# A fused macaron block on one Trainium2 core: second norm of the first feed-forward phase on ScalarE, transposes in halves, k weight split first

## The chip, the cores and the metric

The kernel runs on one core of a Trainium2 chip. The metric is the device time of one execution in microseconds (us). Three runs of the kernel before took 5574.15, 5580.31 and 5580.04 us; their median is 5580.04.

## The reference, cut to what matters

The input x is (4, 2048, 512) in float32. Three blocks follow one another, each on a layer norm of its input:

```python
x = x + 0.5 * ffn(layernorm(x))      # first feed-forward phase
x = x + mixer(layernorm(x))          # state-space block with its own residual
x = x + 0.5 * ffn(layernorm(x))      # second feed-forward phase, same weights
...
def ffn(x):                          # x_prev is x one token earlier, zero at a sequence's start
    xr = mu_r * x + (1 - mu_r) * x_prev
    xk = mu_k * x + (1 - mu_k) * x_prev
    r = sigmoid(xr @ W_r.T)
    k = square(relu(xk @ W_k.T))
    return r * (k @ W_v.T)
```

The mixer returns its output plus its own (normalised) input. So its residual is x1 + h2, where x1 is what the first feed-forward block gives and h2 is the layer norm of x1. The mixer centres its input and multiplies by W_in; then come a short convolution, a selective scan over 16 states and an output product.

## The kernel before

The program has three parts, one after the other: `ffn_phase` named "f1", `mixer_phase`, and `ffn_phase` named "f2". All engines meet at the end of each part. Inside a part each engine runs its own instruction list, written out by hand, and waits on semaphores; an engine executes its list strictly in order. So the order of calls in each engine's function is the schedule.

**A feed-forward phase** handles 16 chunks of 512 tokens (FT; four a sequence). A chunk lies as four tiles of 128 tokens by 512 channels. Its steps, with the engine and the line:

- SP (SyncE) loads x (line 171) and stores the result (197); it also stores h2T, the transposed second norm, for the mixer (204).
- VectorE does `norm1` (343 to 357): statistics, then rstd from POOL (`power`, 223), then the normalised hx. TensorE turns hx (`turn1`, 476) into two PSUM banks `ps_t`, four blocks one after the other, and ScalarE copies each block to xhT (271). POOL takes the difference to the token before (`shift`, 231, one instruction over the whole chunk). VectorE mixes (375), ScalarE makes the rounded high part (278 for xk, 285 for xr), and VectorE the low part (378).
- TensorE makes the products k, r and v, each as three matmuls on high and low parts (509 to 511), 48 for each of k, r and v in a chunk. ScalarE takes relu, square and the high part of k (291 to 295) and the tanh of r (303); VectorE makes k's low part (390), multiplies r by v (422) and adds into x (427). That sum is x1.
- Only in f1: a second norm of x1 on VectorE (343 to 357 again, output h2), the sum x1 + h2 on POOL (247), TensorE's transposes of h2 (`turn2`, 476, all four blocks, through the same two banks) and ScalarE's copies to h2T (333).

The work is software-pipelined. In the body of chunk i TensorE runs v of chunk i, the transposes of hx of chunk i+2, k and r of chunk i+1, and the transposes of h2 of chunk i. VectorE runs x1 and the second norm of chunk i, k's low part of chunk i+1, the xk mix of i+2, norm1 of i+3 and the xr mix of i+2. ScalarE runs the xhT copies (i+2), the k tiles and two r tiles (i+1), xk's high part (i+2), two r tiles (i+1), the four h2T copies (i) and xr's high part (i+2). The last three bodies leave out the chunks that don't exist. In the last body of f1 TensorE and VectorE also centre W_in for the mixer (399, 560); a tile named mx_w_in in the trace can be one that f1 uses as scratch for x, hx, the difference or the mix.

**The prologue** of each phase loads chunk 0 of x, then W_r, W_k and W_v and the two mu vectors (164 to 169). TensorE transposes the three weights block by block into the two `ps_t` banks (466, twelve groups), ScalarE copies out the high part (258) and VectorE subtracts for the low part (406). That happens after the transposes of chunk 0 and ahead of the first mix. The fourth chunk of x is loaded only once all weights are transposed, since W_v waits in its buffer (172).

Of the kernel before, what the change touches and what calls it, by code (L numbers as in the profile page):

```python
# [14 lines left out]
F32 = mybir.dt.float32  # L15
# [35 lines left out]
def ffn_phase(nc, name, x_in, w_r, w_k, w_v, mu_r, mu_k, out, hT_pad=None, ahead=None):  # L51
# [7 lines left out]
    with ExitStack() as ctx:  # L59
# [25 lines left out]
        rstd = sb("rstd", [P, 2, FJ])  # L85
        mark = sb("mark", [P, 1])
# [20 lines left out]
        s_w = sem("weights_loaded")  # L107
# [11 lines left out]
        s_dsh = sem("dsh_ready")  # L119
        s_mk = sem("xk_mixed")  # L120
# [13 lines left out]
        s_xs = sem("xs_ready")  # L134
        s_t2 = sem("h2_transposed")
# [8 lines left out]
        block = ctx.enter_context(nc.Block())  # L144

# [17 lines left out]
        def _(sp):  # L163
            sp.dma_start(x[0][:, :, :], x_v[0]).then_inc(s_x[0], 16)
            for n, w in enumerate((w_r, w_k, w_v)):
                sp.dma_start(w_nat[n], w.rearrange("(o p) c -> p o c", p=P)).then_inc(s_w, 16)
            for n, m in enumerate((mu_r, mu_k)):
                sp.dma_start(mu[:, n, :], m.rearrange("(o p) -> p o", p=P),
                             allow_slow_non_contiguous=True).then_inc(s_w, 16)
# [41 lines left out]
        def _(pool):  # L211
# [42 lines left out]
        def _(act):  # L254
            def copy_weights():
                for g in range(3 * NB):
                    act.wait_ge(s_wt, g + 1)
                    nc.scalar.activation(w_hi[:, g // NB, g % NB, :], ps_t[g % 2][:, :], ACT.Copy).then_inc(s_wh, 1)  # L258
# [28 lines left out]
            def copy_k(i):  # L287

                for d in range(NB):
# [1042 lines left out]
```

## Time and profile before

| what | value |
|---|---|
| runs, us | 5574.15, 5580.31, 5580.04; median 5580.04 |
| the profiled execution's own time | 5575.4 us |
| its span, first to last instruction | 5573.6 us |
| mean granted TensorE clock | 0.990 of full |
| TensorE busy (matmul) | 5397.0 us, 97% |
| VectorE busy | 4949.2 us, 89% |
| POOL busy | 4269.2 us, 77% |
| ScalarE busy | 3482.6 us, 62% |
| first feed-forward phase | 0 to about 706 us |
| mixer | about 706 to 4943 us |
| second feed-forward phase | from about 4943 us |

All times in the rows are microseconds from the start of the span, unless marked ns. A busy engine isn't always at its peak: an instruction that waits for a port or for another engine's hold on it counts as busy too. PE is TensorE, DVE VectorE, ACT ScalarE, POOL GpSimd, SP SyncE; L427 is line 427 of the kernel before.

### The profile page before, as it was taken

The page shows a single profiled execution, that of the slowest core. Times are in us where ns is not written, and L with a number is a line of the kernel's source. Part 1 is how long each engine was busy: PE and PEld are TensorE (multiplying, and loading weights), DVE is VectorE, ACT ScalarE, POOL GpSimd, SP SyncE. Part 2 cuts the span into 40 slices and gives each one's busy share as a digit, 9 for nine tenths or more (in the row PEclk, how much of TensorE's full clock was granted, in tenths as well). Part 3 has the DMA queues.
Part 4 walks back from the last instruction along what each step waited for, and adds up shares of the span by engine and source line. Part 5 has one row for each costly group of instructions (what it writes and reads, how often), then busy time and mean ns, then how long its engine had stood idle before and what let it go on. Part 6 is the DMA issues. An engine that isn't in the chain of part 4 may idle for free. (4 is left out here: it accounts for less than half of the span.)

```text
span 5573.6 us, 82586 instructions
## 1 busy us (share of the span) xinstructions
PE 5397.0 (97%) x23584; PEld 4365.6 (78%) x23584; DVE 4949.2 (89%) x8180; ACT 3482.6 (62%) x8814; POOL 4269.2 (77%) x2671
## 2 busy tenths in 40 slices
PE   7999989999999999999999999999999999979999
PEld 6777768888777788878878888777788888857777
DVE  6888779999999999999999999999999999966775
ACT  4444357677666766766766677666766766744443
POOL 2233269999999999999999999999999999931110
PEclk8999999999999999999999999999999999989999
DMA  2212221111111111111111111111111111121111
GB/s 85 91 68 89 81 103 35 43 50 58 56 44 43 43 43 43 43 43 46 43 43 43 43 51 57 57 43 43 43 43 43 43 43 46 43 95 61 53 53 46
DMA packets 140105, 298.00 MB, mean 53 GB/s; under 512 B 23424, under 2 KB 41888, under 8 KB 139680
## 3 DMA queue, kind: packets, MB, share of 16 engines
q1 hardware_dynamic: 139680, 293.09, 15.4%
q8 instruction: 174, 2.85, 0.2%
q14 instruction: 251, 2.06, 0.1%
HBM read 223.79 MB, written 69.27 MB: 53 GB/s over the span
## 5 line engine op out<-in xcount | busy, mean ns | idle before, releaser
L845 POOL TENSOR_TENSOR mx_dbu<-mx_bs,mx_du 128x1024 f32<-128x1024 f32 x1024 | 2414.8, 2358 | 39.2 <-POOL mx_du L838 28.9
L973 ACT ACTIVATE mx_ps_da<-mx_dl,mx_a 128x256 f32<-128x256 f32 x4096 | 1775.5, 464 | 82.7 <-DVE mx_hp L1052 48.2
L1052 DVE TENSOR_TENSOR_SCAN mx_hp<-mx_ps_da,mx_hst,mx_dbu 128x256 f32<-128x256 f32 x2048 | 1500.8, 733 | 0.3 <-ACT mx_ps_da L973 0.3
L1052 DVE TENSOR_TENSOR_SCAN mx_ps_da<-mx_ps_da,mx_hst,mx_dbu 128x256 f32<-128x256 f32 x2048 | 1416.9, 737 | 11.1 <-ACT mx_ps_da L973 6.1
L826 POOL TENSOR_TENSOR mx_hp<-mx_hp,mx_cs 128x512 f32<-128x512 f32 x1024 | 1303.7, 1273 | 4.1 <-ACT mx_hst L907 4.1
L1207 PE MATMUL mx_ps_y<-mx_hp,mx_ident 128*128 128x256 f32 x4096 | 1054.3, 380 | 0.0
L1198 PE MATMUL mx_ps_y<-mx_hc,mx_ident 128*128 128x256 f32 x4096 | 1051.1, 379 | 0.0
L1174 PE MATMUL mx_ps_m<-mx_u,mx_w_dt 128*128 128x256 f32 x4128 | 936.6, 380 | 5.6 <-issue 5.6
L1207 PEld LDWEIGHTS mx_ps_y<-mx_hp,mx_ident 128*128 128x128 f32 x4096 | 774.0, 190 | 174.6 <-issue 60.4
L1174 PEld LDWEIGHTS mx_ps_m<-mx_u,mx_w_dt 128*128 128x128 f32 x4128 | 786.5, 191 | 113.9 <-issue 6.3
L925 ACT ACTIVATE mx_hst<-mx_ps_da 128x2 f32<-128x2 f32 x1022 | 173.6, 170 | 1103.8 <-DVE mx_hc L1064 1099.7
L1198 PEld LDWEIGHTS mx_ps_y<-mx_hc,mx_ident 128*128 128x128 f32 x4096 | 778.2, 190 | 105.8
L1064 DVE TENSOR_TENSOR mx_hc<-mx_ps_da,mx_cs 128x512 f32<-128x512 f32 x1024 | 688.7, 673 | 137.6 <-PE mx_ps_y L1198 132.2
L1155 PE MATMUL mx_ps_m<-mx_hT,mx_w_in 128*128 128x256 f32 x2072 | 501.6, 385 | 56.6 <-DVE mx_u L1024 56.6
L1147 PE MATMUL mx_ps_m<-mx_hT,mx_w_in 128*128 128x259 f32 x2136 | 514.1, 383 | 5.0 <-PEq L59 3.7
L223 POOL TENSOR_TENSOR f_rstd<-f_ve,f_half 128x4 f32<-128x4 f32 x48 | 48.5, 1011 | 606.5 <-DVE f_ve L352 606.2
L1147 PEld LDWEIGHTS mx_ps_m<-mx_hT,mx_w_in 128*128 128x128 f32 x2136 | 406.1, 190 | 122.6 <-issue 63.6
L1155 PEld LDWEIGHTS mx_ps_m<-mx_hT,mx_w_in 128*128 128x128 f32 x2072 | 390.0, 191 | 135.3 <-DVE mx_u L1024 82.5
L1186 PE MATMUL mx_ps_m<-mx_w_out,mx_gy 128*128 128x512 f32 x1024 | 480.6, 592 | 0.8 <-DVE mx_xo L1043 0.8
L1024 DVE SCALAR_TENSOR_TENSOR mx_u<-mx_ps_m,mx_cw,mx_u 128x256 f32<-128x256 f32 x798 | 379.5, 476 | 18.3
L817 POOL TENSOR_TENSOR mx_dl<-mx_dl,mx_en 128x256 f32<-128x256 f32 x257 | 186.8, 727 | 172.7 <-ACT mx_en L901 171.1
L1186 PEld LDWEIGHTS mx_ps_m<-mx_w_out,mx_gy 128*128 128x128 f32 x1024 | 194.5, 190 | 138.9 <-issue 124.1
(107 smaller groups left out, 6745.1 us busy)
## 6 DMA issues: line engine op xcount, KB each, us to landing
mx_bs<-bc_scratch SPq DMA_DIRECT2D x132, 512.0 KB, 3.7
mx_cs<-bc_scratch SPq DMA_DIRECT2D x132, 512.0 KB, 3.9
mx_hT<-hT_scratch SPq DMA_DIRECT2D x34, 518.0 KB, 3.9
hT_scratch<-f_h2T SPq DMA_DIRECT2D x16, 1024.0 KB, 5.1
mx_xo<-xs_scratch SPq DMA_DIRECT2D x32, 512.0 KB, 5.1
x_scratch<-mx_xo SPq DMA_DIRECT2D x32, 512.0 KB, 5.1
f_x<-x_scratch SPq DMA_DIRECT2D x16, 1024.0 KB, 5.7
out_dram<-f_x SPq DMA_DIRECT2D x16, 1024.0 KB, 4.2
```

Of the source, the lines that this page charges most:

```text
L826: G.tensor_tensor(h, h, cs[:, g, SD:SG, :], ALU.mult).then_inc(s_pr, 1)
L845: G.tensor_tensor(dbu[:, n % NM], bs[:, g], bcast(du[:, b % 2, :], SG), ALU.mult).then_inc(s_m1, 1)
L973: ins = A.activation(ps_da[DA_BANK[p]][:, k, :], dl[:, b % NL, :], ACT.Exp, scale=a_sb[:, b, s:s + 1])
L1024: V.scalar_tensor_tensor(out=q, in0=in_bank(b)[:, step:step + T], scalar=cw[:, step, b:b + 1], in1=q, op0=ALU.mult, op1=ALU.add).then_inc( ...
L1052: ins = V.tensor_tensor_scan(da if half == 0 else hp[:, n % NH, k, :], da, dbu[:, n % NM, s, :], hst[:, b, SG * g + s:SG * g + s + 1], ALU ...
L1064: V.tensor_tensor(hc[:, n % NC, :, :], ps_da[DA_BANK[2 * n]][:, :, :], cs[:, g, 0:SD, :], ALU.mult).then_inc(s_m2, 1)
L1147: ins = M.matmul(in_bank(b)[:, 0:TH], w_in_sb[:, f, b * P:(b + 1) * P], hT[cp][:, f, :], start=(f == 0), stop=(f == NB - 1))
L1155: ins = M.matmul(m_bank(b)[:, 0:T], w_in_sb[:, f, DI + b * P:DI + (b + 1) * P], hT[cp][:, f, PAD_L:PAD_L + T], start=(f == 0), stop=(f == ...
L1174: ins = M.matmul(m_bank(b)[:, 0:T], w_dt_sb[:, k, b * P:(b + 1) * P], u[:, cp, k, :], start=(k == 0), stop=(k == ND - 1))
L1186: ins = M.matmul(ps_c[:, :], gy[:, cp, b, j * P:(j + 1) * P], w_out_sb[:, b, :], start=(b == 0), stop=(b == ND - 1), skip_group_check=True)
L1198: ins = M.matmul(ps_y[b % 2][:, 0:T], ident[:, :], hc[:, n % NC, k, :], start=(g == 0 and k == 0), stop=False, skip_group_check=True)
L1207: ins = M.matmul(ps_y[b % 2][:, 0:T], ident[:, :], hp[:, n % NH, k, :], start=False, stop=(g == NG - 1 and k == SG - SD - 1), skip_group_c ...
```

## The change

In both phases the k weight is loaded and split first, ahead of the transposes of chunk 0. Two of the r weight's blocks are transposed before k's first two tiles and two after them; the v weight comes after k's last tile. The shift, the xk mix and its rounding are done block by block for chunk 0. The mu loads stand ahead of those of W_r and W_v on SP's queue. In the first phase VectorE computes only the statistics of the second norm and two small factors, shift2 = -mean x rstd and gain2 = rstd + 1. ScalarE computes h2 = rstd x x1 + shift2, and in place x = gain2 x x1 + shift2, which is x1 + h2. POOL's sum is gone. The transposes of h2 come in two halves, one between r's second and third tile, one after r's last. In the last body ScalarE makes the sum last.

```diff
+        shift2 = sb("shift2", [P, FJ])
+        gain2 = sb("gain2", [P, FJ])
...
+        W_ORDER = (1, 0, 2)
+        def groups(nth, of=range(NB)):
+            return [(NB * nth + o, W_ORDER[nth], o) for o in of]
...
-            for n, w in enumerate((w_r, w_k, w_v)):
-                sp.dma_start(w_nat[n], w.rearrange("(o p) c -> p o c", p=P)).then_inc(s_w, 16)
+            sp.dma_start(w_nat[1], w_k.rearrange("(o p) c -> p o c", p=P)).then_inc(s_w[1], 16)
             for n, m in enumerate((mu_r, mu_k)):
                 sp.dma_start(mu[:, n, :], m.rearrange("(o p) -> p o", p=P),
-                             allow_slow_non_contiguous=True).then_inc(s_w, 16)
+                             allow_slow_non_contiguous=True).then_inc(s_mu, 16)
+            sp.dma_start(w_nat[0], w_r.rearrange("(o p) c -> p o c", p=P)).then_inc(s_w[0], 16)
+            sp.dma_start(w_nat[2], w_v.rearrange("(o p) c -> p o c", p=P)).then_inc(s_w[2], 16)
...
                 pool.wait_ge(s_tc, NB * (i + 1))
                 pool.wait_ge(s_prev, i + 1)
-                if not (isinstance(i, int) and i == 0):
-                    pool.wait_ge(s_xr, i)
+                pool.wait_ge(s_xr, i)
                 nc.gpsimd.tensor_tensor(dsh[:, :, :], xhT[:, slot, :, 1:FT + 1], xhT[:, slot, :, 0:FT],
                                         ALU.subtract).then_inc(s_dsh, 1)
+            def first_shift():
+                pool.wait_ge(s_prev, 1)
+                for f in range(NB):
+                    pool.wait_ge(s_tc, f + 1)
+                    nc.gpsimd.tensor_tensor(dsh[:, f, :], xhT[:, 0, f, 1:FT + 1], xhT[:, 0, f, 0:FT],
+                                            ALU.subtract).then_inc(s_dsh0, 1)
             def prologue():
                 power(0, 0)
-                shift(0, 0)
+                first_shift()
...
-                    pool.wait_ge(s_h2, FJ * (i + 1))
-                    nc.gpsimd.tensor_tensor(x[c][:, :, :], x[c][:, :, :], h2[:, :, :], ALU.add).then_inc(s_xs, 1)
...
-            def copy_weights():
-                for g in range(3 * NB):
+            def copy_weights(nth, of=range(NB)):
+                for g, n, o in groups(nth, of):
                     act.wait_ge(s_wt, g + 1)
-                    nc.scalar.activation(w_hi[:, g // NB, g % NB, :], ps_t[g % 2][:, :], ACT.Copy).then_inc(s_wh, 1)
+                    nc.scalar.activation(w_hi[:, n, o, :], ps_t[o % 2][:, :], ACT.Copy).then_inc(s_wh, 1)
+            def first_high_xk():
+                for f in range(NB):
+                    act.wait_ge(s_mk, f + 1)
+                    nc.scalar.activation(xk_hi[:, f, :], mix[:, f, :], ACT.Copy).then_inc(s_hi0, 1)
...
+            def second_norm(i, c):
+                act.wait_ge(s_nb, i + 1)
+                for j in range(FJ):
+                    nc.scalar.activation(h2[:, j, :], x[c][:, j, :], ACT.Identity, bias=shift2[:, j:j + 1],
+                                         scale=rstd[:, 1, j:j + 1]).then_inc(s_h2, 1)
+            def add_second_norm(i, c):
+                for j in range(FJ):
+                    ins = nc.scalar.activation(x[c][:, j, :], x[c][:, j, :], ACT.Identity, bias=shift2[:, j:j + 1],
+                                               scale=gain2[:, j:j + 1])
+                ins.then_inc(s_xs, 1)
+            def copy_h2T(i, blocks):
+                for f in blocks:
+                    act.wait_ge(s_t2, NB * i + f + 1)
+                    nc.scalar.activation(h2T[:, f, 0:FT], ps_t[f % 2][:, :], ACT.Copy).then_inc(s_t2c, 1)
             def prologue():
                 act.wait_ge(s_id, 3)
+                copy_weights(0)
                 copy_xhT(0, 0, True)
-                copy_weights()
-                high_xk(0)
+                first_high_xk()
+                copy_weights(1, range(2))
                 high_xr(0)
-                copy_k(0)
+                copy_k(0, range(2))
+                copy_weights(1, range(2, NB))
+                copy_k(0, range(2, NB))
+                copy_weights(2)
                 copy_xhT(1, 1, False)
                 high_xk(1)
...
                     copy_k(i + 1)
+                if mixer:
+                    second_norm(i, c)
                 if left == 0 or left > 1:
                     copy_r(i + 1, range(2))
+                if mixer:
+                    if left != 1:
+                        add_second_norm(i, c)
+                    act.wait_ge(s_ht, (2 * BATCH + 1) * 16 + 16 * i)
+                    copy_h2T(i, range(2))
                 if left == 0 or left > 2:
                     high_xk(i + 2)
                 if left == 0 or left > 1:
                     copy_r(i + 1, range(2, FJ))
                 if mixer:
-                    act.wait_ge(s_ht, (2 * BATCH + 1) * 16 + 16 * i)
-                    for f in range(NB):
-                        act.wait_ge(s_t2, NB * i + f + 1)
-                        nc.scalar.activation(h2T[:, f, 0:FT], ps_t[f % 2][:, :], ACT.Copy).then_inc(s_t2c, 1)
+                    copy_h2T(i, range(2, NB))
+                    if left == 1:
+                        add_second_norm(i, c)
                 if left == 0 or left > 2:
                     high_xr(i + 2)
...
+            def split_weights(nth, of=range(NB)):
+                for g, n, o in groups(nth, of):
+                    dve.wait_ge(s_wh, g + 1)
+                    V.tensor_tensor(w_lo[:, n, o, :], ps_t[o % 2][:, :], w_hi[:, n, o, :].bitcast(F32),
+                                    ALU.subtract).then_inc(s_wc, 1)
+            def first_mixed_k():
+                dve.wait_ge(s_mu, 2 * 16)
+                for f in range(NB):
+                    dve.wait_ge(s_dsh0, f + 1)
+                    V.scalar_tensor_tensor(out=mix[:, f, :], in0=dsh[:, f, :], scalar=mu[:, 1, f:f + 1],
+                                           in1=xhT[:, 0, f, 0:FT], op0=ALU.mult, op1=ALU.add).then_inc(s_mk, 1)
+                for f in range(NB):
+                    dve.wait_ge(s_hi0, f + 1)
+                    ins = V.tensor_tensor(xk_lo[:, f, :], mix[:, f, :], xk_hi[:, f, :].bitcast(F32), ALU.subtract)
+                ins.then_inc(s_xk, 1)
             norm1(0, 0, 0, 1)
-            dve.wait_ge(s_w, 5 * 16)
-            for g in range(3 * NB):
-                dve.wait_ge(s_wh, g + 1)
-                V.tensor_tensor(w_lo[:, g // NB, g % NB, :], ps_t[g % 2][:, :],
-                                w_hi[:, g // NB, g % NB, :].bitcast(F32), ALU.subtract).then_inc(s_wc, 1)
-            mixed_k(0, 0)
+            split_weights(0)
+            first_mixed_k()
+            split_weights(1, range(2))
             mixed_r(0, 0)
+            split_weights(1, range(2, NB))
             norm1(1, 1, 1, 1)
+            split_weights(2)
             split_k(0)
             mixed_k(1, 1)
             norm1(2, 2, 2, 1)
...
-                    def free():
-                        if left in (1, 2):
-                            dve.wait_ge(s_t2, NB * i)
-                            dve.wait_ge(s_xs, i)
-                    norm(1, x[c], h2, norms_before_2(i, left), s_h2, free)
+                    statistics(1, x[c], norms_before_2(i, left))
+                    if not (isinstance(i, int) and i == 0):
+                        dve.wait_ge(s_xs, i)
+                    V.scalar_tensor_tensor(out=shift2[:, :], in0=mv[:, 1, :, 0], scalar=-1.0, in1=rstd[:, 1],
+                                           op0=ALU.mult, op1=ALU.mult)
+                    V.tensor_scalar(gain2[:, :], rstd[:, 1], 1.0, None, ALU.add).then_inc(s_nb, 1)
...
-            def turn_weights():
-                for g in range(3 * NB):
-                    if g >= 2:
+            def turn_weights(nth, of=range(NB)):
+                for g, n, c in groups(nth, of):
+                    if c == 0:
+                        pe.wait_ge(s_w[n], 16)
+                    if c >= 2 or nth == 2:
                         pe.wait_ge(s_wc, g - 1)
-                    else:
-                        pe.wait_ge(s_tc, NB)
+                    elif nth == 1:
+                        pe.wait_ge(s_tc, NB - 1 + c)
                     for o in range(NB):
-                        ins = M.transpose(ps_t[g % 2][:, o * P:(o + 1) * P],
-                                          w_nat[g // NB][:, o, (g % NB) * P:(g % NB + 1) * P], ident[:, :])
+                        ins = M.transpose(ps_t[c % 2][:, o * P:(o + 1) * P],
+                                          w_nat[n][:, o, c * P:(c + 1) * P], ident[:, :])
                     ins.then_inc(s_wt, 1)
...
+                    elif isinstance(i, int) and i < 2:
+                        pe.wait_ge(s_wc, (2 * i + 1) * NB - 1 + f)
...
+                turn_weights(0)
                 turn1(0)
-                pe.wait_ge(s_w, 5 * 16)
-                turn_weights()
-                k_products(0)
+                turn_weights(1, range(2))
+                k_products(0, range(2))
+                turn_weights(1, range(2, NB))
+                k_products(0, range(2, NB))
+                turn_weights(2)
...
-                    r_products(i + 1)
+                    r_products(i + 1, range(2))
                 if mixer:
-                    turn2(i)
+                    turn2(i, range(2))
+                if left == 0 or left > 1:
+                    r_products(i + 1, range(2, FJ))
+                if mixer:
+                    turn2(i, range(2, NB))
```

## Rows read from the trace of the kernel before

**Rows 1.** Busy time by stretch: start:end, length, then per engine busy and count, clock, DMA.

```profile
core 0: us, PE busy (x) PEld busy (x) DVE busy (x) ACT busy (x) POOL busy (x), PEclk, DMA share, GB/s
123.55:161.85 38.30, 37.73 (x177) 30.42 (x176) 30.40 (x51) 17.98 (x27) 11.73 (x4) 1.00 0.22 83
...
279.40:319.74 40.34, 37.71 (x177) 30.43 (x176) 33.75 (x51) 17.78 (x27) 12.41 (x4) 1.00 0.21 78
...
5100.46:5136.42 35.96, 35.71 (x163) 28.75 (x161) 25.29 (x37) 15.84 (x23) 4.61 (x2) 1.00 0.17 59
85.30:645.60 560.30, 532.95 (x2459) 429.85 (x2458) 461.81 (x686) 249.86 (x377) 170.36 (x55) 0.99 0.21 77
```

**Rows 2.** Timeline of TensorE: start, length, engine, line, operation, operands, count, idle before.

```profile
304.13 1.04 PE L476 MATMUL f_ps_t<-f_ident,f_h 128*128 128x128 f32 x8
307.54 1.15 PE L476 MATMUL f_ps_t<-f_ident,f_h 128*128 128x128 f32 x8 [2.37 <-ACT f_h2T L333]
308.44 0.47 PE L509 MATMUL f_ps_v<-f_w_lo,f_ka_hi 128*128 128x512 f32 x1
...
319.76 1.04 PE L476 MATMUL f_ps_t<-f_ident,mx_w_in 128*128 128x128 f32 x8
...
321.95 0.47 PE L509 MATMUL f_ps_kr<-f_xk_lo,f_w_hi 128*128 128x512 f32 x1
```

**Rows 3.** Timeline of VectorE over the same body.

```profile
288.54 2.47 DVE L346 BATCH_NORM_STATS2 f_stats<-f_x 128x6 f32<-128x512 f32 x4
...
291.46 0.17 DVE L352 TENSOR_SCALAR f_ve<-f_mv 128x4 f32<-128x4 f32 x1
292.75 1.92 DVE L356 TENSOR_SCALAR f_h<-f_x,f_mv,f_rstd 128x512 f32<-128x512 f32 x4 [1.12 <-POOL f_rstd L223]
...
297.00 7.08 DVE L375 SCALAR_TENSOR_TENSOR mx_w_in<-mx_w_in,f_mu,f_xhT 128x512 f32<-128x512 f32 x4
...
321.40 2.47 DVE L422 SCALAR_TENSOR_TENSOR f_rt<-f_rt,f_ps_v 128x512 f32<-128x512 f32 x4
323.91 4.95 DVE L427 SCALAR_TENSOR_TENSOR f_x<-f_rt,f_x 128x512 f32<-128x512 f32 x4
```

**Rows 4.** Timeline of POOL over the same body.

```profile
294.75 6.79 POOL L247 TENSOR_TENSOR f_x<-f_x,f_h 128x2048 f32<-128x2048 f32 x1 [2.03 <-DVE f_h L356]
...
322.90 3.60 POOL L231 TENSOR_TENSOR mx_w_in<-f_xhT 128x2048 f32<-128x2048 f32 x1 [10.46 <-ACT f_xhT L271]
```

**Rows 5.** Timeline of ScalarE over the same body.

```profile
294.36 0.64 ACT L295 ACTIVATE f_ka_hi<-f_ka 128x512 fp32r<-128x512 f32 x1
...
304.11 1.91 ACT L278 ACTIVATE f_xk_hi<-mx_w_in 128x2048 fp32r<-128x2048 f32 x1 [4.82 <-DVE mx_w_in L375]
```

**Rows 6.** Groups of ScalarE, whole run: shapes, count, busy, mean ns, idle before.

```profile
L973 ACT ACTIVATE mx_ps_da<-mx_dl,mx_a 128x256 f32<-128x256 f32 x4096 | 1775.5, 464 | 82.7 <-DVE mx_hp L1052 48.2
...
L901 ACT ACTIVATE mx_en<-mx_en 128x256 f32<-128x256 f32 x258 | 103.2, 400 | 0.1
...
L303 ACT ACT_TABLE_LOAD x1 | 1.3, 1283 | 0.0
```

**Rows 7.** Chain that ended last, prologue of the second phase: start, length, what.

```profile
4959.85 0.65 PE f_ps_t L466 x4
...
4974.27 2.66 DVE f_mix L375 x4
...
4981.24 0.80 PE f_ps_kr L509
...
4999.38 3.61 POOL f_dsh L231
...
5009.72 0.80 PE f_ps_kr L509
```

**Rows 8.** Timeline of SP's queue, first mu load of the second phase.

```profile
4946.28 2.23 SPq L168 DMA_DIRECT2D f_mu<-in_L_ffn_mu_r  x1
```

**Rows 9.** Timeline of POOL at the end of the first phase.

```profile
699.73 4.55 POOL L247 TENSOR_TENSOR f_x<-f_x,f_h 128x2048 f32<-128x2048 f32 x1 [2.03 <-DVE f_h L356]
705.92 0.20 POOL L809 MEMSET mx_ident<- 128x128 f32 x1 [1.65 <-POOLq L59]
```

More of the change, by code:

```diff
@@ L106, in ffn_phase @@
         s_id = sem("ident_made")
-        s_w = sem("weights_loaded")
+        s_w = [sem(f"weight_loaded{n}") for n in range(3)]
+        s_mu = sem("mu_loaded")
         s_x = [sem(f"x_loaded{n}") for n in range(NX)]
@@ L119, in ffn_phase @@
         s_dsh = sem("dsh_ready")
+        s_dsh0 = sem("first_dsh_ready")
+        s_hi0 = sem("first_mix_high_ready")
         s_mk = sem("xk_mixed")
@@ L134, in ffn_phase @@
         s_xs = sem("xs_ready")
+        s_nb = sem("second_norm_factors_ready")
         s_t2 = sem("h2_transposed")
@@ L285, in high_xr, with copy_k @@
                 nc.scalar.activation(xr_hi[:, :, :], mix[:, :, :], ACT.Copy).then_inc(s_hi, 1)
-            def copy_k(i):
-                for d in range(NB):
+            def copy_k(i, tiles=range(NB)):
+                for d in tiles:
                     act.wait_ge(s_kr, 2 * NB * i + d + 1)
@@ L341, in _, with statistics @@
             V = nc.vector
-            def norm(which, src, dst, k, done, before):
+            def statistics(which, src, k):
                 st = 2 * FJ * k
@@ L353, in norm @@
                 dve.wait_ge(s_rs, k + 1)
+            def norm(which, src, dst, k, done, before):
+                statistics(which, src, k)
                 before()
@@ L367, in mixed @@
             def mixed(i, slot, n, lo, hi, done, low):
-                dve.wait_ge(s_dsh, i + 1)
+                if isinstance(i, int) and i == 0:
+                    dve.wait_ge(s_dsh0, NB)
+                else:
+                    dve.wait_ge(s_dsh, i)
                 if n == 0:
@@ L376, in mixed @@
                                            in1=xhT[:, slot, f, 0:FT], op0=ALU.mult, op1=ALU.add).then_inc(done, 1)
-                dve.wait_ge(s_hi, 2 * i + 2 - n)
+                dve.wait_ge(s_hi, 2 * i + 1 - n)
                 V.tensor_tensor(lo[:, :, :], mix[:, :, :], hi[:, :, :].bitcast(F32), ALU.subtract).then_inc(low, 1)
@@ L456, in _, with turn @@
             M = nc.tensor
-            def turn_weights():
-                for g in range(3 * NB):
-                    if g >= 2:
+            def turn_weights(nth, of=range(NB)):
[3 more added lines that the diff above has]
+                    if c >= 2 or nth == 2:
                         pe.wait_ge(s_wc, g - 1)
-                    else:
-                        pe.wait_ge(s_tc, NB)
+                    elif nth == 1:
+                        pe.wait_ge(s_tc, NB - 1 + c)
                     for o in range(NB):
-                        ins = M.transpose(ps_t[g % 2][:, o * P:(o + 1) * P],
-                                          w_nat[g // NB][:, o, (g % NB) * P:(g % NB + 1) * P], ident[:, :])
+                        ins = M.transpose(ps_t[c % 2][:, o * P:(o + 1) * P],
+                                          w_nat[n][:, o, c * P:(c + 1) * P], ident[:, :])
                     ins.then_inc(s_wt, 1)
-            def turn(i, src, ready, done, copied_before):
+            def turn(i, src, ready, done, copied_before, blocks=range(NB)):
                 pe.wait_ge(ready, FJ * (i + 1))
-                for f in range(NB):
+                for f in blocks:
                     copied_before(f)
@@ L482, in bank, with turn2 @@
                         pe.wait_ge(s_tc, NB * i + f - 1)
+                    elif isinstance(i, int) and i < 2:
+                        pe.wait_ge(s_wc, (2 * i + 1) * NB - 1 + f)
                     elif mixer and not (isinstance(i, int) and i < 3):
                         pe.wait_ge(s_t2c, NB * (i - 2))
-                    elif not (isinstance(i, int) and i == 0):
+                    else:
                         pe.wait_ge(s_tc, NB * i)
                 turn(i, hx, s_hx, s_t, bank)
-            def turn2(i):
+            def turn2(i, blocks=range(NB)):
                 def bank(f):
@@ L498, in bank @@
                         pe.wait_ge(s_tc, NB * (i + 3))
-                turn(i, h2, s_h2, s_t2, bank)
+                turn(i, h2, s_h2, s_t2, bank, blocks)
             def bank_free(n, first):
@@ L512, in split_product, with k_products @@
                 return ins
-            def k_products(i):
+            def k_products(i, tiles=range(NB)):
                 pe.wait_ge(s_xk, i + 1)
-                for d in range(NB):
+                for d in tiles:
                     bank_free(2 * NB * i + d, isinstance(i, int) and i == 0 and d < 2)
@@ L521, in k_products, with r_products @@
                     ins.then_inc(s_kr, 1)
-            def r_products(i):
+            def r_products(i, tiles=range(FJ)):
                 pe.wait_ge(s_xr, i + 1)
-                for j in range(FJ):
+                for j in tiles:
                     bank_free(2 * NB * i + NB + j, False)
```

## The prediction, made before the changed kernel was run

> **What bounds the kernel now.** I cut the trace into stretches of one feed-forward body each (one 512-token chunk). In the first phase a body took 38.30 us early on and 40.34 us later; from the third chunk's transposes to the end of the fifteenth's products (14 bodies) it is 560.30, or 40.02 a body. A body of the second phase takes 35.96 and has no second norm [rows 1]. TensorE's timeline of one body [rows 2] shows what its floor is: the body from 279.40 to 319.76 consists of the transposes of hx (2.2), 96 products of k and r (the rest, 22.5), the transposes of h2 (304.13 to 308.44, 4.3, of which 2.37 waiting for ScalarE) and 48 products of v (11.3). The second burst of eight transposes takes 0.90 to the next product. So without waits the floor is near 38.
>
> VectorE sets the 40.34. Busy 33.75 of 40.34 there [rows 1], the other 6.6 are round trips (to POOL for rstd, to ScalarE for the rounded high part) that its own queue imposes; it never waits for v (321.40 carries no wait [rows 3]). The expensive row is the first mix after the second norm, four instructions in 7.08 us, where the same four take 2.66 with POOL idle [rows 3, 7]. It lies over POOL's residual sum, 294.75 to 301.54 [rows 4]: the first of them ends only when POOL is through. The x1 sum (4.95, beginning 323.91) is held in the same way by POOL's shift, 322.90 to 326.50 [rows 3, 4]. Early bodies are shorter because VectorE still has its head start.
>
> **The body, part by part.** Removed from VectorE: four normalising instructions on h2 (292.75, 1.92 [rows 3]). Removed from POOL: the 6.79 sum, and with it 7.08 - 2.66 = 4.42 of VectorE. Added on VectorE: two 128x4 instructions; one that exists (291.46) takes 0.17 [rows 3], I take 0.2 each. VectorE then needs 40.36 - 1.92 - 4.42 + 0.4 = 34.4, under TensorE's 38.
>
> ScalarE gets eight 128x512 instructions with a scale and a bias taken from memory. None like it is in the trace. Without such operands a 128x512 one takes 0.64 [rows 5]; at 128x256 one with a scale from memory takes 0.464 against 0.400 without [rows 6]. So below 0.64, above 0.64 + 2 x 0.1 = 0.84; I take 0.72 each, since instructions in a row overlap a little, 2.9 for four. The Trainium skill, "ScalarE: Activation LUTs", section "Rules for kernel authors", says to put add and mul on VectorE, not on ScalarE. By that rule the move loses, 2.9 against 1.92 for the norm; it leaves out that ScalarE is busy only 17.8 of 40.34 [rows 1] and that the sum comes off POOL.
>
> Now the order, in us after T, TensorE's start on the transposes of hx(i+2):
> - ScalarE has evacuated the last k tile at 15.6 (294.36 + 0.64 - 279.40) [rows 5]. The factors of the second norm are there by then: even if VectorE starts its x1 work late at 3.3, POOL's shift holds its sum to 7.0, the sum ends 9.5, rstd 4.2 later (288.54 to 292.75 [rows 3]), factors at 14.1. h2 is written 15.6 to 18.5; TensorE wants it after the second r tile, at 19.1.
> - the second r tile leaves TensorE at 2.2 + 22.5 x 6/8 = 19.1 and is evacuated by 19.9; the residual sum 19.9 to 22.8, two h2T copies to 23.9, then xk's high part, 23.9 to 25.8. Queued behind the sum are those copies and the rounding, and VectorE, ready with its mix at 19, now waits 5 us for the latter instead of 2.
> - VectorE: from xk's rounding to the next x1 work is 17.3 (304.11 to 321.40 [rows 3, 5]), so 41.2, or 3.3 in the next body, which is what I began with. hx is ready at 34.2, needed at 38.
> - TensorE: r tiles 2 and 3 run while ScalarE copies the first half of h2T, so the 2.37 wait is gone. Floor: 2.2 + 22.5 + 11.3 + 2 x 0.90 + 0.1 for one more switch = 37.95.
>
> POOL's queue now holds only the shift and the two rstd. SP's stores of x wait for the sum at 22.8 where before it ended at 301.54 - 279.40 = 22.1: nothing waits for them so closely. 14 bodies: 14 x (37.95 - 40.02) = **-29.0 us**. The next stage is thin: the loop ScalarE rounding, VectorE, factors, ScalarE again is 17.3 + 2.5 + (shift, sum) 3.7 to 5.0 + 4.2 + 0.4 + 2.9 + 1.1 + 2.9 + 1.1 = 36.1 to 37.4, only 0.5 to 1.9 below 37.95.
>
> **The prologues.** In the second phase twelve weight tiles go through TensorE, ScalarE and VectorE in turn, 4959.85 to 4974.27, 1.2 each; only then comes the mix, and k's products begin at 4981.24 [rows 7]. In the new order w_k's four tiles go first, two of them while the first norm runs; its last is split near 4959.3, so the transposes of x start 3 us later. Shift and mix, now per block, end near 4966.5 (POOL and VectorE take turns), rounding and low parts near 4969.4: k's products begin 12 us earlier. But the eight tiles of w_r and w_v are only moved. Two are split behind xk's low part, two after xr, whose ScalarE copies stand behind the k evacuations (near 4980), then norm1(1) to 4987.5, then w_v's four to 4990.5, with TensorE mostly idle. Only then is a transpose bank free for x's second chunk: the shift at 4999.38 moves to about 4993.6. From there on the chain (shift, mix, high, table load, r's evacuation, products again at 5009.72 [rows 7]) is unchanged. So 12 us become **-5.8**. Bounds: 0, if a wait for w_v takes it all, and -12. On SP's queue the two mu loads pass w_r and w_v, which are issued 4.8 later (2.23 for the one [rows 8]), still before their use at 4962 and 4984; the load of x's fourth chunk waits for w_v's transposes, some 15 us later, and is needed 40 us after that. The first phase has the same prologue: **-5.8** again.
>
> **The end of the first phase.** Before, POOL's last sum (699.73, 4.55) ends at 704.28 and the mixer begins at 705.92 [rows 9]. Now in a row: h2 on ScalarE (698.1 to 701.0), transposes and copies to 704.3, then the sum to 707.2: **+2.9**; nothing hides it, since all engines meet there. Bounds +1.5 and +4.
>
> **Sum.** -29.0 - 5.8 - 5.8 + 2.9 = -37.7. The profiled execution's own time is 5575.4 (span 5573.6): 5537.7. The median of the runs shown is 4.6 higher, 5580.0, which gives 5542.3. I take 5539, nearer to the former, whose level one of the three runs (5574.2) has too.
>
> **The rivals** (on the scale of the 5539).
> 1. *The prologues bring nothing.* The products start earlier but the moved tiles hold up x's second chunk as long as before. For it: 12 us of the 14.4 are only moved. Against: VectorE idles before 4961 and in four round trips. Then -29.0 + 2.9: 5551.
> 2. *ScalarE and VectorE become the bound.* If the eight instructions take 0.84, or POOL's shift is late by another us, the loop above passes 37.95; it decides from 0.5 us on. At 39.3 a body the gain there is 10: -10 - 11.6 + 2.9, 5558.
> 3. *Slower: table loads.* If the new function shares no table set with Tanh, each body gets loads before h2, before the r tiles, before the sum: 3 x 1.28 [rows 6] in the loop, 37.4 + 3.85, and TensorE waits another 0.7 for h2: 42.0 a body. 14 x 1.98 - 11.6 + 2.9 + 1.3 = +20: 5597. It decides from 40.5 a body. Against: Copy, Relu, Square and Tanh run through the phase with one single load at L303 in the second phase [rows 6]. The Trainium skill, same page, section "Table sets", says identity, like copy and relu, is in every set; by that the rival falls. The trace can't show it for this function.
>
> **Chances.** Forecast 0.69, prologues nothing 0.12, loop bound 0.16, table loads 0.03. A measurement of this kernel tells about 0.2% (11 us) from no change. Faster 0.94: the first three, less a little where both 1 and 2 hold; same 0.03; slower 0.03. The range: prologues at -12 each give 5524; loop bound 5558; 5522 to 5560 leaves out table loads and combinations.
>
> **What would show it.** Bodies of the first phase at 38.0, TensorE without a wait inside the h2 transposes, all at full granted clock; the mix at 2.7 where 7.08 stood; ScalarE's eight at 0.65 to 0.85; VectorE waiting 4 to 6 for xk's rounding; k's first products 12 us and the second shift 6 us earlier in each phase; the mixer 32 us earlier. Wrong if a body stays over 39, if table loads appear in it, or if ScalarE is late with h2.

## The result, and the profile after

Median **5540.5 us** (5539.1 to 5542.5, 4 runs) against 5578.3 (5574.2 to 5580.3) in the same session: ratio 0.9933, interval 0.9916 to 0.9951. The profiled execution took 5539.1 with a span of 5536.8, against 5575.4 and 5573.6. The prediction was 5539, range 5522 to 5560.

By stage, in the profiled executions. The mixer begins with the load of w_dt on SP's queue (at 706.80 before, 675.26 after), the second phase with the load of its first x (4943.35 before, 4911.92 after).

| | before | after | difference |
|---|---|---|---|
| start to the third chunk's transposes | 85.3 | 77.8 | -7.5 |
| 14 bodies [rows 1] | 560.3 | 534.2 | -26.1 |
| from there to the mixer | 61.2 | 63.3 | +2.1 |
| mixer | 4236.6 | 4236.7 | 0 |
| second phase | 630.3 | 624.9 | -5.4 |

Busy time by stretch of the changed kernel, columns as in [rows 1]: the 14 bodies, one body, a body whose chunk is the first of a batch row, a body of the second phase.

```profile
77.78:612.00 534.22, 524.00 (x2463) 425.18 (x2462) 370.43 (x658) 321.91 (x489) 77.75 (x41) 1.00 0.24 79
118.89:156.84 37.95, 37.41 (x177) 30.38 (x177) 26.55 (x49) 22.97 (x35) 5.62 (x4) 1.00 0.26 84
194.81:234.05 39.24, 37.73 (x178) 30.44 (x178) 27.85 (x51) 23.08 (x35) 5.62 (x4) 1.00 0.25 81
5100.46:5136.42 35.96, 35.71 (x162) 28.77 (x161) 24.98 (x37) 15.84 (x23) 4.61 (x2) 1.00 0.17 59
```

A body is 37.95 where TensorE is busy 37.41, three of them are 39.24, and VectorE has fallen from 33.75 [rows 1] to 26.55. TensorE's waits over the bodies (us in total, times, longest):

```profile
PE f_ps_t L549 <- ACT f_xhT L292: 6.1, 13, 0.6
PE f_ps_v L584 <- DVE f_xk_lo L435: 3.8, 3, 1.3
```

The waits for h2's copies [rows 2] are gone. What is left is 0.54 us in most bodies for ScalarE's copy of hx (the normalised x), and in three bodies a wait for xk's low part ahead of v's products. VectorE, the same body as in [rows 3]:

```profile
271.68 2.47 DVE L495 SCALAR_TENSOR_TENSOR f_rt<-f_rt,f_ps_v 128x512 f32<-128x512 f32 x4
274.19 3.70 DVE L500 SCALAR_TENSOR_TENSOR f_x<-f_rt,f_x 128x512 f32<-128x512 f32 x4
...
282.21 0.17 DVE L510 TENSOR_SCALAR f_gain<-f_rstd 128x4 f32<-128x4 f32 x1
...
285.05 2.73 DVE L432 SCALAR_TENSOR_TENSOR mx_w_in<-mx_w_in,f_mu,f_xhT 128x512 f32<-128x512 f32 x4
294.31 2.29 DVE L435 TENSOR_TENSOR f_xk_lo<-mx_w_in,f_xk_hi 128x2048 fp32r<-128x2048 f32 x1 [6.52 <-ACT f_xk_hi L299]
```

The mix that took 7.08 takes 2.73; after it VectorE waits 6.52 for the rounded xk. ScalarE [rows 5]:

```profile
284.31 2.92 ACT L330 ACTIVATE f_h<-f_x,f_shift,f_rstd 128x512 f32<-128x512 f32 x4
287.14 0.58 ACT L324 ACTIVATE f_rt<-f_ps_kr 128x512 f32<-128x512 f32 x1
288.09 0.60 ACT L324 ACTIVATE f_rt<-f_ps_kr 128x512 f32<-128x512 f32 x1 [0.37 <-PE f_ps_kr L586]
288.58 2.92 ACT L336 ACTIVATE f_x<-f_x,f_shift,f_gain 128x512 f32<-128x512 f32 x4
291.41 1.06 ACT L344 ACTIVATE f_h2T<-f_ps_t 128x512 f32<-128x512 f32 x2
292.37 1.91 ACT L299 ACTIVATE f_xk_hi<-mx_w_in 128x2048 fp32r<-128x2048 f32 x1
```

Four instructions with scale and bias from memory take 2.92, and no table load (ScalarE's load of function tables) stands between them. The Trainium skill, "ScalarE: Activation LUTs", section "What ACT_TABLE_LOAD costs", has 186 ns + 0.833 ns a column, about 93 ns more for each such operand and 93 ns of overlap in a row: an estimate of 0.80 for the first and 0.71 for each further one, 2.92 for four. The trace agrees.

In the second phase's prologue k's first products, the second chunk's shift and the restart of r's products [rows 7]:

```profile
4937.64 0.80 PE L584 MATMUL f_ps_kr<-f_xk_lo,f_w_hi 128*128 128x512 f32 x1 [5.68 <-DVE f_xk_lo L473]
...
4962.98 3.60 POOL L242 TENSOR_TENSOR f_dsh<-f_xhT 128x2048 f32<-128x2048 f32 x1 [8.82 <-ACT f_xhT L292]
...
4973.31 0.80 PE L584 MATMUL f_ps_kr<-f_w_lo,f_xr_hi 128*128 128x512 f32 x1 [5.45 <-ACT f_rt L324]
```

The phase starts at 4911.92, 31.4 earlier than before. Against that start k's products are 12.2 earlier, the shift 5.0 and r's restart 5.0.

### The profile page after: what moved, and what is told of

Read it like the earlier page. It is cut to its first block and busy times, and to the rows that moved or that the text cites. A ratio compares the mean times of both kernels' runs of the same rounds, so it can differ in the third digit from the quotient of the medians.

```text
span 5536.8 us, 82707 instructions
## 1 busy us (share of the span) xinstructions
PE 5386.1 (97%) x23584; PEld 4361.7 (79%) x23584; DVE 4854.1 (88%) x8154; ACT 3566.5 (64%) x8948; POOL 4168.6 (75%) x2661
```

## The experiments

The baseline is the changed kernel unless a run says otherwise. The numbers in brackets behind a median are its ratio to the kernel before in the same session, with the interval. "First phase" is the time to the mixer's first load, and stage times are those of the profiled executions. The runs fall in four sessions, in which the kernel before took 5579.7 (the first four kernels, to the transposes whole), 5575.1 (no xk wait, the longer chains, the last sum on VectorE), 5580.5 (w_v late, the last sum on VectorE with four copies, all together) and 5582.0 (the body alone with four copies). A difference between medians of two sessions can be off by some 5 us by that alone, so the stage times carry the argument there.

**The body alone, the prologue alone.** One kernel has the old prologue and the new body, the other the new prologue and the old body.

> The prologues of the kernel before with the bodies and the end of the changed one. Theory (the two parts add up): first-phase bodies near 38.0 us with VectorE free of POOL's sum, the second shift of each phase where it was before (51 us after the first norm begins), the end of the first phase 3 us longer; in all 25 us below before, near 5551. Rival (the bodies are only short because the new prologue gives VectorE a head start): bodies drift back towards 40 as they did before, gain under 12 us.

> The prologues of the changed kernel with the bodies and the end of the kernel before. Theory: k's first products 12 us earlier, the second shift 5 to 7 us earlier in each phase, all of it kept to the end of the phase: 12 us below before in all, near 5564. Rival (in the first phase, where VectorE sets the pace of the later bodies, the gain is lost again, since VectorE's own list is what counts there): 5 to 6 us below before, all from the second phase.

Body alone: 5561.0 (0.9965, interval 0.9951 to 0.9978); first phase 683.2, 23.6 less than before, with bodies of 37.95 and three of 39.25, so the rival (bodies drift back to 40) is out; but its mixer took 10 us more than the kernel before's and the changed kernel's, which later runs take up. Prologue alone: 5569.3 (0.9982, 0.9973 to 0.9991), 10.4 less than before in the medians and 7.5 in the profiled executions; second phase -6.4, first phase only -1.35, as the rival had it. There the third chunk's shift was nearly as early as with both parts (81.76 against 81.02, and 88.54 before), and the 13 bodies after it, 40.6 on the mean, gave the start back. TensorE's waits and a piece of POOL's and VectorE's timelines in the kernel with the prologue alone:

```profile
PE f_ps_t L548 <- ACT f_h2T L380: 24.9, 13, 2.5
```

```profile
293.91 6.80 POOL L265 TENSOR_TENSOR f_x<-f_x,f_h 128x2048 f32<-128x2048 f32 x1 [2.03 <-DVE f_h L407]
296.15 7.10 DVE L429 SCALAR_TENSOR_TENSOR mx_w_in<-mx_w_in,f_mu,f_xhT 128x512 f32<-128x512 f32 x4
```

So the parts don't add: 23.6 and 1.35 apart, 31.5 together. With the old bodies, which VectorE paces, the head start is used up; with the new ones it is kept.

**The residual sum back on POOL**, h2 still on ScalarE.

```
+ pool.wait_ge(s_h2, FJ * (i + 1))
+ nc.gpsimd.tensor_tensor(x[c], x[c], h2, ALU.add)
- add_second_norm(i, c)        (ScalarE, both places)
```

> The changed kernel with the residual sum back on POOL and h2 still made by ScalarE. Theory A (as in the prediction's sum: POOL's hold costs VectorE 4.4 us a body wherever it falls): VectorE needs 38.8 to 39.3 a body and sets the pace, 12 to 19 us slower than the changed kernel. Theory B (with h2 made later, POOL's sum now runs 19 to 25 us into the body, while VectorE waits for ScalarE's rounding anyway, and ScalarE gets to that rounding 2.9 us earlier): bodies stay at 37.95, the end of the phase is 1 us shorter, no difference over 2 us from the changed kernel.

5529.7 (0.9913, 0.9898 to 0.9928), **10.8 less than the changed kernel**; first phase 666.0, -9.3; bodies 37.67 throughout; mixer and second phase within 0.6 of the changed kernel's. Theory A is out. Theory B has the place of POOL's sum right, but neither expected a gain. VectorE and POOL in it:

```profile
282.89 2.74 DVE L430 SCALAR_TENSOR_TENSOR mx_w_in<-mx_w_in,f_mu,f_xhT 128x512 f32<-128x512 f32 x4
289.35 2.91 DVE L433 TENSOR_TENSOR f_xk_lo<-mx_w_in,f_xk_hi 128x2048 fp32r<-128x2048 f32 x1 [3.72 <-ACT f_xk_hi L301]
```

```profile
285.15 4.95 POOL L265 TENSOR_TENSOR f_x<-f_x,f_h 128x2048 f32<-128x2048 f32 x1 [5.21 <-ACT f_h L332]
```

```profile
PE f_ps_t L547 <- ACT f_xhT L294: 3.3, 13, 0.3
```

POOL's sum now begins 0.5 before the end of the mix, where before it began 2.25 ahead of the mix [rows 3, 4], and lies in VectorE's wait for xk. It holds only xk's low part, which started 0.75 before the sum's end and took 2.91 instead of 2.29. The Trainium skill, "SBUF — State Buffer", section "SBUF: two separate sides", says that the port pair VectorE and GpSimd share is an exclusive lock kept for a whole instruction. The trace agrees: the 0.62 more of xk's low part is near the 0.75 that it overlapped, and what the sum costs VectorE hangs on where it begins, 4.4 us in the old place and 0.6 here. The 9.3 us are three xk waits (3.8), 0.28 in each of 14 bodies (3.9) and 2.3 at the end of the phase, less a prologue 0.5 later (9.5 by these terms).

**h2's transposes whole** (48 products of r, then all of h2; ScalarE's four copies stand together behind r's last tiles).

```
- r_products(i + 1, range(2)); turn2(i, range(2))
- r_products(i + 1, range(2, FJ)); turn2(i, range(2, NB))
+ r_products(i + 1); turn2(i)
```

> The changed kernel with the transposes of h2 in one piece behind r's last tile. Theory: TensorE waits about 0.8 us for ScalarE's copies between the two pairs of blocks, bodies of 38.6 instead of 37.95, less the wait for xk ahead of v in every fourth body, which goes: 4 to 9 us slower than the changed kernel. Rival (the wait of 2.37 us seen before was the lack of halves): 40.3 a body, 30 us slower. Second rival (the halves do nothing): within 1 us.

5542.7 (0.9934, 0.9919 to 0.9949), +2.2; first phase +2.75; bodies 38.25.

```profile
PE f_ps_t L548 <- ACT f_h2T L344: 4.3, 14, 0.3
```

0.3 a body, not the 2.37 of [rows 2] and not the 0.8 of the theory. Before, ScalarE's copies of h2T stood behind xk's rounding, which had waited 4.82 for VectorE's long mix and began only at 304.11 [rows 5], with TensorE's transposes begun at 304.13. With the mix done in time the wait is small without halves too; with the old body and its long mix it is there again, 24.9 in 13 (the kernel with the prologue alone). The halves are worth little.

**No wait for xk ahead of v.** The case `if c == 0: pe.wait_ge(s_xk, i + 2)` is left out.

> The changed kernel without TensorE's wait for xk ahead of v in a sequence's first body (s_ka, which it also waits for, already stands behind VectorE's use of the banks). Theory: the three bodies of 39.24 us in the first phase become 37.95, 3.8 us less; the second phase doesn't change. Rival: the wait only uncovers the next one (ScalarE's evacuation or the shift), under 1 us.

5536.4 (0.9936, 0.9922 to 0.9951), -4.1, which the ratios (0.9936 against 0.9933) do not bear out; first phase -2.5. All bodies are 37.95 (37.86 to 38.04), so the three waits are gone (-3.9); the second chunk's shift is 0.8 later in this execution and the end of the phase 0.5 longer. This kernel is the base of the experiments that follow, but for the body alone with four copies.

**ScalarE's chain longer**, by one and by two roundings of xk (1.91 each).

```
+ nc.scalar.activation(xk_hi, mix, ACT.Copy)     (once, or twice)
+ act.wait_ge(s_ex, ...)                          (so that they run one after the other)
```

> The kernel of no_xk_wait with xk's rounding done twice on ScalarE (1.9 us more in each body of both phases, same output). Theory (the loop ScalarE, VectorE, factors, ScalarE takes 35.7 to 37.4 in the first phase and TensorE's floor is 37.95): the loop comes to 37.6 to 39.3, bodies of 37.95 to 38.6, 0 to 9 us slower than no_xk_wait; the second phase, which has no such loop, stays at 35.96. Rival (ScalarE's time is covered whatever its place, it is busy 23 of 38): no difference. Rival (ScalarE's chain already sets the pace): 1.9 a body, 27 us slower.

> The kernel of no_xk_wait with xk's rounding done three times (3.8 us more in each body). Theory: the loop comes to 39.5 to 41.2, first-phase bodies of 39.5 to 41, 20 to 43 us slower than no_xk_wait, and about 1.9 a body more than with one repetition once that one is past the floor. Rival (covered): no difference in either.

5581.2 (1.0013, 1.0004 to 1.0023) and 5661.8 (1.0162, 1.0145 to 1.0178): +44.8 and +125.4. The first phase takes 40.6 and 85.4 more, the second 3.8 and 37.4. Both theories had slack in the first phase, and **there is none**: the rival that ScalarE's chain already sets the pace has the wait right. And both kept the second phase at 35.96, but its bodies take 36.1 with one rounding more and 38.0 to 39.6 with two, so the same chain is there as well, with about 1.7 us of slack. ScalarE and TensorE in the first phase of the first kernel:

```profile
281.95 1.91 ACT L309 ACTIVATE f_xr_hi<-mx_w_in 128x2048 fp32r<-128x2048 f32 x1 [9.27 <-DVE mx_w_in L435]
283.77 0.19 ACT L290 ACTIVATE f_xhT<-f_xhT 128x4 f32<-128x4 f32 x1
283.87 1.06 ACT L293 ACTIVATE f_xhT<-f_ps_t 128x512 f32<-128x512 f32 x2
```

```profile
284.50 1.60 PE L552 MATMUL f_ps_t<-f_ident,mx_w_in 128*128 128x128 f32 x8 [2.49 <-ACT f_xhT L293]
...
285.75 0.78 PE L587 MATMUL f_ps_kr<-f_xk_lo,f_w_hi 128*128 128x512 f32 x1
286.32 0.63 PE L588 MATMUL f_ps_kr<-f_xk_hi,f_w_hi 128*128 128x512 f32 x1
...
288.44 0.39 PE L587 MATMUL f_ps_kr<-f_xk_lo,f_w_hi 128*128 128x512 f32 x1
```

Ahead of the copies of hx in ScalarE's queue stands the rounding of xr, which waits for VectorE's second mix, and that for xk's rounding. In the base kernel the rounding of xr is over 0.85 after TensorE begins its transposes, and TensorE waits 0.54 for the copy:

```profile
PE f_ps_t L549 <- ACT f_xhT L292: 7.0, 13, 0.6
```

The least that TensorE waits there is 0.25 (the POOL kernel). With 1.91 more in the chain the wait is 2.49: all of it arrives (+1.95). The bodies in which the clock stays up take 39.90, which is 37.95 and the 1.91, so 37.95 is the length of the loop itself. On top, after nine of the thirteen such waits, the products behind the wait take 0.63 instead of 0.39, at a granted clock of 0.50 (1.2 GHz) for 2.7 us and 1.00 after it; such a body takes 1.5 us more, and all 13 take 40.9 on the mean:

```profile
285.70:288.40 2.70, 2.70 (x8) 2.18 (x7) 2.70 (x5) 0.72 (x2) 1.59 (x1) 0.50 0.00 0
289.00:300.00 11.00, 11.00 (x49) 8.84 (x48) 8.82 (x19) 7.06 (x12) 2.42 (x2) 1.00 0.00 0
```

**The last chunk's sum on VectorE.**

```
- if left == 1: add_second_norm(i, c)
+ V.tensor_scalar(x[c][:, j, :], ..., gain2, shift2, mult, add)  x4  (VectorE, left == 1)
```

> The kernel of no_xk_wait with the last body's residual sum on VectorE, behind the centring of W_in, where it overlaps ScalarE's copies of h2T. Theory: the first phase ends 2.5 to 2.9 us earlier (ScalarE's sum at 669.8 to 672.7 goes, VectorE has its own done by 670): 2.6 us less than no_xk_wait. Rival: the copies and the store of h2T end it anyway, under 1 us.

5541.4 (0.9943, 0.9929 to 0.9957): +4.9. The first phase is 2.9 shorter (669.9 against 672.8), as expected; the mixer is 10.8 longer. In two stretches of it VectorE waits for ScalarE, and ScalarE for nothing that the profile shows:

```profile
2788.68 0.40 ACT L984 ACTIVATE mx_en<-mx_en 128x256 f32<-128x256 f32 x1
...
2795.41 0.17 ACT L1008 ACTIVATE mx_hst<-mx_ps_da 128x2 f32<-128x2 f32 x1 [6.32 <-issue]
```

```profile
2797.62 0.17 DVE L1163 MEMSET mx_hst<- 128x128 f32 x1 [6.72 <-ACT mx_hst L1008]
```

The same gap is 1.60 in the base kernel, ended by VectorE. ScalarE's waits in the mixer (us in total, times, longest):

```profile
ACT mx_hst L1008 <- issue: 13.2, 2, 6.9
```

**The same, with four 128x4 copies added** on ScalarE at the start of the first phase; and the body-alone kernel with the same four.

```
+ for k in range(4): nc.scalar.activation(pad[:, 4*k:4*k+4], ident[:, 0:4], ACT.Copy)
```

> The kernel with the last chunk's sum on VectorE, which gained its 2.9 us at the end of the first phase and lost 10.8 in the mixer, where ScalarE shows two stretches of 6.3 and 6.9 us ended by nothing that the profile shows, each ahead of the same instruction (the first copy of the state). Four 128x4 copies are added on ScalarE at the start of the first phase, as many instructions as the last chunk's sum had there. Theory A: those stalls hang on where an instruction lies in ScalarE's program; with the count restored they are gone, and the kernel takes 5536.4 - 2.9 + 0.5 = 5534. Theory B: they hang on when the mixer begins or differ from execution to execution; then they stay and the time is 5541 to 5542.

> The kernel with the new body and the old prologue (5560.98 median, 5554.94 to 5565.65), whose mixer was 10 us longer than in the kernels around it, with ScalarE stalls of 5.3 and 6.2 us that end on nothing the profile shows; and four 128x4 copies added on ScalarE at the start of the first phase, as in the run that cured the kernel with its last sum on VectorE (stalls 13.2 in all down to 5.8, mixer 4246.6 down to 4236.1). Theory A, the place of an instruction in ScalarE's program: any such shift changes the stalls, here most likely back under 3 us each, mixer near 4236, time 5551. Theory B, execution by execution: stalls of 5 to 7 us stay in some executions, median 5558 to 5563. If the time is 5551, the new body alone is worth -29 of its own as in my sum, and the prologue the rest.

In this order: 5530.9 (0.9911, 0.9894 to 0.9927), mixer 4236.1 instead of 4246.6; and 5553.9 (0.9947, 0.9934 to 0.9961), mixer 4237.2 instead of 4246.6. The stalls, first the kernel with the last sum on VectorE:

```profile
ACT mx_hst L1012 <- issue: 5.8, 2, 3.3
```

and the body-alone kernel without and with the copies:

```profile
ACT mx_hst L957 <- issue: 11.5, 2, 6.2
```

```profile
ACT mx_hst L961 <- issue: 5.0, 2, 2.6
```

With four instructions added that do nothing useful the medians are 10.4 and 7.0 lower, and the mixers 10.5 and 9.4 shorter. Stalls of up to some 3 us cost little (mixers of 4236.1 to 4239.1, against 4234.8 to 4236.8 without any), those of 5 to 7 cost 10 in all. Theory A expected them gone, and they are halved. The runs speak for it but don't show it: a trace holds one execution, each kernel and its version with the copies ran in different sessions on different chips, and the kernel without the xk wait shows no such stall and the changed kernel two (5.4), though only TensorE's program differs between them. The body alone is worth 23.0 us in the first phase with the copies (23.6 without), and the last sum on VectorE 2.9 there; the 5.5 between the medians 5536.4 and 5530.9 are of two sessions.

Where the stalls lie can be read. Every kernel's mixer runs the first batch row in line and the other three in a loop (`Fori(1, BATCH)`), so the program goes back to the loop's start twice, for the third and the fourth row. In the changed kernel the first copy of the state in the second, third and fourth row is this:

```profile
1750.87 0.15 ACT L1007 ACTIVATE mx_hst<-mx_ps_da 128x2 f32<-128x2 f32 x1
...
2799.26 0.17 ACT L1007 ACTIVATE mx_hst<-mx_ps_da 128x2 f32<-128x2 f32 x1 [2.23 <-issue]
...
3844.57 0.17 ACT L1007 ACTIVATE mx_hst<-mx_ps_da 128x2 f32<-128x2 f32 x1 [3.12 <-issue]
```

The stalls stand at the two returns, and none stands where the loop is entered from the first row.

**w_v turned behind x's second chunk**, in both phases.

```
- turn_weights(2); turn1(1); r_products(0)
+ turn1(1); turn_weights(2); r_products(0)    (ScalarE likewise; VectorE splits w_v behind k's low part)
```

> The kernel without TensorE's wait for xk (36.41 median, 5536.4), and w_v turned only after x's second chunk, in both phases. My prediction said that w_r's and w_v's eight tiles hold up x's second chunk, so that 12 us of earlier k products become 5.8. If w_v's four tiles are what stands ahead of it, they took 3 us there (my 4987.5 to 4990.5), which go behind it, into the time in which TensorE waits for the second mix: shift of chunk 1 some 3 us earlier in each phase, 5530.5 in all. The rival: the stretch behind is a chain through VectorE (norm of x's chunk 1, its mix), which has waited for nothing on TensorE, and the splits of w_v then fall into it: same time, 5536.4, or 1 to 2 us worse.

5530.2 (0.9911, 0.9894 to 0.9927), -6.2. The second chunk's shift in the first phase is at 48.21 instead of 51.20, and the first phase 3.8 shorter; in the second phase that shift is 3.8 earlier, and the phase 6.0 shorter; the mixer is 2.3 longer, with one stall of 2.8. So w_v's four tiles did hold x's second chunk, by the 3 us of my estimate or a little more.

**All that helped, together**: POOL's sum, no xk wait, w_v late, and r's first two tiles evacuated ahead of xk's rounding in the prologue.

> Together: POOL keeps the residual sum (5529.7 with it, 10.8 less than the changed kernel), TensorE does not wait for xk ahead of v, w_v is turned behind x's second chunk, and r's first two tiles are evacuated ahead of xk's rounding in the prologue (TensorE waits 4.04 us for one of them in the first phase of the changed kernel). The xk wait brings nothing here, since with POOL's sum the bodies had none of it (37.67 each). w_v late 3 us a phase if it holds in its own run, the earlier evacuation 3 to 4 us a phase: 5529.7 - 6 - 7 = 5517. The rival: VectorE's chain (norm, mix) sets the second half of the prologue and both edits bring nothing: 5530. Against the mixer's stalls on ScalarE nothing is done; if they fall to 6 us each, 10 us are added to either.

**5519.5** (5519.1 to 5522.0; ratio 0.9892, 0.9875 to 0.9908): 61 us less than before, 21 less than the changed kernel. Its bodies:

```profile
75.67:565.21 489.54, 486.28 (x2289) 395.08 (x2288) 378.03 (x625) 266.64 (x403) 137.45 (x53) 1.00 0.25 82
113.25:150.90 37.65, 37.40 (x177) 30.40 (x177) 29.05 (x49) 20.50 (x31) 10.56 (x5) 1.00 0.25 85
```

Against the kernel with POOL's sum the first phase is 5.9 shorter and the second 6.9, the mixer 1.9 longer: of 13 us expected 10.2 came. The early evacuation did less than its 3 to 4 a phase: against the kernel with w_v late alone the second phase is 1.3 shorter. TensorE's wait for that tile, 4.0 and 5.4 in the two phases when w_v is early, was only 0.95 and 2.4 with w_v late, so most of it had gone already.

## Why the prediction was right, and where it was not

- **The sum.** -37.7 predicted, -36.3 in the profiled executions, -37.8 in the medians. No rival came at its price, but the total is nearer than its terms: by stage they miss by +2.9, -1.7, +0.4 and -0.8, which cancel in good part. That is luck. A slip without effect: prologues at -12 each give 5527 on the scale of the 5539, not 5524.
- **The bodies, -29.0: measured -26.1.** The term left out the order of ScalarE's work against TensorE's wait ahead of v. With the sum ahead of xk's rounding, xk's low part is late in the three bodies that wait for it: 3.9 us. Leaving the wait out gives them back.
- **"The floor is 37.95", and "the loop is 0.5 to 1.9 below": both wrong, by 0.3 and more, in opposite directions.** A body bound by TensorE is 37.65 (the last kernel); the 37.95 of the changed kernel holds a wait of 0.54, 0.3 more than it must, and is the length of the loop. That the floor of my forecast and the loop as measured share this number is luck; the floor's own terms add up to 37.9. I followed the loop through VectorE's x1 work back to ScalarE, and left out what it passes on the way: the rounding of xr, and behind it in ScalarE's queue the copies of hx that TensorE needs at the start of the next body. So rival 2, the loop as the bound, was there already, at its edge; I had given it 0.16 and a slack of 0.5 us before it decides. The longer chains showed that it decides from nothing: 1.91 us added to the loop made bodies of 39.90 at full clock, and cost 44.8 in all with the lower clock and the second phase.
- **Removing POOL's hold of 4.42 from VectorE.** The 7.08 went to 2.73 as predicted, but not because the sum left POOL. With the sum on POOL again the mix still takes 2.74. It is the order that did it: h2 on ScalarE comes later in VectorE's body, and the sum, which needs h2, with it. The part of the change that moves the sum to ScalarE costs 9.3 us of the first phase; the part that moves the norm earns the gain. So the cause that the prediction gave for 4.42 of VectorE's time was wrong, and its number right by luck.
- **Transposes in halves, TensorE's 2.37 wait.** The wait is gone as predicted, but the halves are not why: with whole transposes it comes back at 0.3 only. It had come from the long mix, by way of xk's late rounding.
- **Prologues, -5.8 each: measured -7.5 and -5.4.** The reason given held: w_v's tiles stand ahead of x's second chunk, and with them behind it the phases are 3.8 and 6.0 shorter still. What the text did not say is that the first phase keeps this gain only with the new bodies: with the old ones 1.35 of it was left.
- **End of the first phase, +2.9: +2.1** from the end of the fifteenth's products. It is ScalarE's last sum: with the sum on POOL the end is 2.3 shorter, and with it on VectorE the first phase is 2.9 shorter.
- **ScalarE's instructions, 2.9 for four: 2.92. Table loads: none. VectorE's wait of 4 to 6 for xk: 6.52.**

## What to carry to other kernels

When work moves to an idle engine, follow that engine's queue past the moved work to the next thing that each other engine takes from it; busy share says nothing of slack (ScalarE was busy 23 us of 38 here and had none), and a loop over several engines has to be closed through every wait it passes. Before taking work off an engine because it blocks another, see whether it can be made to start a little later: here the same sum on the same engine costs VectorE 0.6 us instead of 4.4 when it begins at the end of the mix. A gain ahead of a loop can be used up by the bodies behind it, as it was here with the old ones, so measure parts of a change together as well as apart.

## What the runs showed of the hardware that was not expected

In two kernels whose mixer is the same text as before's, ScalarE stopped in the mixer for 5 to 7 us with nothing to wait for that the profile shows, twice in the traced execution, each time where the loop over batch rows goes back to its start; with four tiny instructions put in some 2800 us earlier the stalls were about 3 us, and the medians 7 to 10 us lower. The Trainium skill, "Runtime: NRT & Kernel Launch", section "Instruction fetch mechanics", says that an engine fetches its program in blocks and that a taken branch out of the blocks it holds makes it wait for a fetch. The place of the stalls, and that they changed with the program's length, fit that; no run shows a fetch itself, and why kernels with equal ScalarE text differ (none, and 5.4) stays open. Whatever the cause, 10 us between two variants of this kernel can come from code that neither of them changes, so a stage-by-stage comparison has to stand beside the total.
